# Graph network, one core: float32 rows turned whole, and no dense slot in the attention

## What is computed

```python
m = MLP(concat(x[dst], x[src] - x[dst]))          # 64 -> 64 -> 128 -> 64 -> 32, relu
x = layernorm(x + segment_mean(m, dst))
x = layernorm(x + segment_sum(x[src] * norm[src] * norm[dst], dst))      # no weights
x = layernorm(x + relu(norm_dst * segment_sum((x * norm_src)[src], dst) @ W + b))
for 3 layers:                                     # attention, 8 heads of 32
    e = leaky_relu((x @ Wl)[src] + (x @ Wr)[dst], 0.2)
    p = segment_softmax(sum(e * att), dst)        # per head
    x = batchnorm(mean_heads(segment_sum(p * (x @ Wl)[src], dst)) + bias (+ act) + x)
x = layernorm(x + ...)
```

## Time and profile before

| | us |
|---|---|
| median of 3 timed runs (5984.18 to 5997.32) | 5986.88 |
| span of the recorded execution | 7770.9 |
| PE busy (matmuls), share of the span | 5760.6 (74%) |
| POOL busy, share | 4059.1 (52%) |
| DVE busy, share | 3565.2 (46%) |
| ACT busy, share | 1748.7 (23%) |
| idle of POOL before attention gathers (2340) | 2221.5 |

### The profile page before, as it was taken

The page is one execution under the profiler, slowest core; times in us unless marked ns, Lnnn a source line. Parts: engine busy times, 40 slices in busy tenths (PEclk is TensorE's granted clock), DMA queues, the critical chain, the costliest instruction groups (busy, mean ns, idle before and its releaser), DMA issues.

```text
span 7770.9 us, 130521 instructions
## 1 busy us (share of the span) xinstructions
PE 5760.6 (74%) x43965; PEld 3691.2 (48%) x43965; DVE 3565.2 (46%) x6811; ACT 1748.7 (23%) x3748; POOL 4059.1 (52%) x4236
## 2 busy tenths in 40 slices
PE   5888886566646666578887876877787758788777
PEld 4666665455545454334444443444444424444444
DVE  5444444455544444444444444444444534444446
ACT  2222222344420000022222221222222122222221
POOL 4555554666646566455555533555555245555551
PEclk8888887777767776688888897888888878888988
DMA  4444443222212222233333332333333223333332
GB/s 103 129 129 129 128 128 98 51 56 56 56 47 56 55 56 55 49 82 93 88 91 88 89 85 56 90 90 89 92 89 89 80 58 92 89 89 93 91 88 65
DMA packets 688913, 648.23 MB, mean 83 GB/s; under 512 B 401396, under 2 KB 483771, under 8 KB 688251
## 3 DMA queue, kind: packets, MB, share of 16 engines
q1 hardware_dynamic: 548266, 463.96, 20.0%
q0 software_dynamic: 135616, 175.22, 11.8%
q10 hardware_dynamic: 4368, 0.70, 0.1%
HBM read 550.21 MB, written 89.17 MB: 82 GB/s over the span
## 4 chain that ended last, share of the span: by engine, by line
PE 43%; issue 22%; another core or an unknown queue 21%; DVE 9%; ACT 3%; DVEq 2%; DMA 0%; POOL 0%; ACTq 0%; POOLq 0%
PE ps L1055 14%; PE ps L900 7%; PE ps L994 5%; PE ps L1005 2%; PE ps L1015 2%; PE ps L855 2%; PE ps L915 1%; PE ps L980 1%; DVE region L1778 1%; DVE acc L1803 1%; PE ps L974 1%; PE ps L864 1%; ACT region L662 1%; PE ps L811 1%
## 5 line engine op out<-in xcount | busy, mean ns | idle before, releaser
L381 POOL DMA_INDIRECT rows<-table,idx x2340 | 2258.3, 965 | 2221.5 <-ACT region L651 1042.6
L1055 PE MATMUL ps<-region,hot 128*128 128x272 f32 x4992 | 1528.3, 457 | 295.8 <-DVE region L1756 159.4
L1055 PEld LDWEIGHTS ps<-region,hot 128*128 128x128 f32 x4992 | 1040.8, 219 | 690.9 <-issue 461.8
L1803 DVE TENSOR_TENSOR acc<-acc,ps 128x272 f32 x1248 | 544.5, 436 | 1685.6 <-remote 808.6
L662 ACT ACTIVATE region<-ps 128x512 f32<-128x512 f32 x1248 | 677.3, 595 | 2691.7 <-remote 1438.8
L900 PE MATMUL ps<-hot,region 128*128 128x192 bf16 (+1 forms) x6144 | 896.1, 309 | 444.2 <-issue 429.0
L900 PEld LDWEIGHTS ps<-hot,region 128*128 128x128 bf16 x6144 | 703.4, 123 | 590.9 <-issue 529.9
L368 POOL DMA_INDIRECT rows<-table,idx x728 | 696.6, 957 | 534.2 <-PE ps L835 320.4
L994 PE MATMUL ps<-xT,wcat 64*128 64x512 f32 x2496 | 771.8, 696 | 170.4 <-issue 92.1
L1778 DVE TENSOR_TENSOR region<-ps,region 128x1056 f32<-128x1056 f32 x582 | 724.7, 1251 | 44.0 <-issue 40.4
L398 POOL DMA_INDIRECT rows<-table,idx x576 | 546.6, 949 | 378.5 <-issue 157.3
(11 more groups left out here) (304 smaller groups left out, 6646.9 us busy)
## 6 DMA issues: line engine op xcount, KB each, us to landing
hot<-hot_dram SPq DMA_DIRECT2D x624, 256.0 KB
turned<-turned_dram SPq DMA_DIRECT2D x624, 128.0 KB
rows<-table,idx POOLq DMA_INDIRECT x3644
hot_dram<-hot SPq DMA_DIRECT2D x104, 512.0 KB
xwin<-table SPq DMA_DIRECT2D x1664, 24.0 KB
region<-hot_dram SPq DMA_DIRECT2D x64, 512.0 KB
region<-d_dram SPq DMA_DIRECT2D x104, 256.0 KB
turned_dram<-turned SPq DMA_DIRECT2D x104, 256.0 KB
```

The costliest lines, as they stand in the source:

```text
L381: pool.indirect_dma_start(rows[:, n % 2, j, :], None, table, bass.IndirectOffsetOnAxis(ap=idx[:, s:s + 1], axis=0)).then_inc(rows_in3[n % ...
L1055: mm = pe.matmul(ps[:, sum_bank(k, side, i), 0:PC + H], hot[:, b, 4 * side + 2 * i + j, :], px[b][:, 4 * side + 2 * i + j, :], start=(j == ...
L1803: v.tensor_tensor(at, at, ps[:, sum_bank(k, side, i), 0:PC + H], ALU.add).then_inc(att_added, 1)
```

## The change

- The rows that are gathered are plain float32: 32 channels, 128 B. In the edge network they come from the input `x`, in layer l of the attention from a new array `feats[l]` that SP stores as soon as x is given. The table keeps the three bfloat16 parts alone (`TAB` 80 to 48 words), for the windows, the dense reads and the convolution; ACT's copy into it goes.
- `rows` becomes a ring of 4 buffers (RING) of 8 places of 64 words: 32 channels and 32 zeros, cleared once by DVE. A slot j stands at `place(j)`, so that slots j and j + 4 lie side by side. One float32 transpose of 128 x 128 turns both sides of one slot pair onto their partitions and zeros between; four turn a group (`turn_rows`). After them the 12 window matmuls (`turn_windows`) write the partitions between, sides alternating.
- The dense slot of the attention goes: no `read_one`, `stationary_one`, `pick_one`, `numbers_for` there; POOL gathers 8 slots in each group. That of the edge network stays; DVE puts it straight into `rows`.
- In the edge network the gathers of group g wait for the turning of g - 4. In the attention they wait for the copy (`xs_kept`) of group n - 4 and, as before, for the turning (`x_made`) of n - 2.
- `x_made` and `x0_made` count 3 for a group in place of 4.

```diff
-TAB = C + 3 * C // 2
+TAB = 3 * C // 2
+RING = 4
+TURN = 3
...
-TURNS = [x for i in range(2) for x in [("row", 2 * i, 0), ("window", i, 0), ("row", 2 * i, 1), ("row", 2 * i, 2), ("window", i, 1),
-                                       ("row", 2 * i + 1, 0), ("row", 2 * i + 1, 1), ("window", i, 2), ("row", 2 * i + 1, 2)]]
+WINDOWS = [(side, i, s) for i in range(2) for s in range(3) for side in range(2)]
...
-        rows = sb("rows", [P, 3, 8, TAB])
+        rows = sb("rows", [P, RING, 8, 2 * C])
...
+        def place(j):
+
+            return 2 * (j % 4) + j // 4
...
         def pool_edges(pool):
 
-            pool.wait_ge(table_stored, 16)
+            pool.wait_ge(rows_cleared, 1)
             for g in range(G):
-                if g >= 3:
-                    pool.wait_ge(x0_made, 4 * (g - 2))
+                if g >= RING:
+                    pool.wait_ge(x0_made, TURN * (g - RING + 1))
                 for j in range(7):
                     pool.indirect_dma_start(
-                        rows[:, g % 3, j, :], None, table,
-                        bass.IndirectOffsetOnAxis(ap=idx[:, 8 * g + j:8 * g + j + 1], axis=0)).then_inc(gathered[g % 3], 16)
+                        rows[:, g % RING, place(j), 0:C], None, x,
+                        bass.IndirectOffsetOnAxis(ap=idx[:, 8 * g + j:8 * g + j + 1], axis=0)).then_inc(rows_at[g % RING], 16)
 
         def pool_attention(pool, l):
 
-            pool.wait_ge(table_stored, 16 * (l + 4))
+            pool.wait_ge(feats_stored, 16 * (l + 1))
             for g in range(G):
                 n = l * G + g
+                if n >= RING:
+                    pool.wait_ge(xs_kept, n - RING + 1)
                 if n >= 2:
-                    pool.wait_ge(x_made, 4 * (n - 1))
-                    pool.wait_ge(xs_kept, n - 1)
-                for j, s in enumerate(piece_slots(g)[0:8 - g % 2]):
+                    pool.wait_ge(x_made, TURN * (n - 1))
+                for j, s in enumerate(piece_slots(g)):
                     pool.indirect_dma_start(
-                        rows[:, n % 2, j, :], None, table,
-                        bass.IndirectOffsetOnAxis(ap=idx[:, s:s + 1], axis=0)).then_inc(rows_in3[n % 2], 16)
+                        rows[:, n % RING, place(j), 0:C], None, feats[l],
+                        bass.IndirectOffsetOnAxis(ap=idx[:, s:s + 1], axis=0)).then_inc(rows_at[n % RING], 16)
...
             for l in range(LAYERS):
+                sp.wait_ge(x_given, 3 + l)
+                sp.dma_start(feats[l].rearrange("(w p) c -> p w c", p=P), X[:, :, :]).then_inc(feats_stored, 16)
                 store_table(sp, 3 + l)
...
+        def turn_rows(pe, bank, b, made):
+
+            for j in range(4):
+                mm = pe.transpose(ps[:, bank, j * P:(j + 1) * P], rows[:, b, 2 * j:2 * j + 2, :].rearrange("p a c -> p (a c)"),
+                                  ident[:, :])
+            mm.then_inc(made, 1)
+
+        def turn_windows(pe, bank, b, made):
+
+            for side, i, s in WINDOWS:
+                q = 64 * side
+                mm = pe.matmul(ps[q + C:q + 2 * C, bank, 2 * i * P:2 * (i + 1) * P], xwin[:, b, 2 * side + i, s * C:(s + 1) * C],
+                               turned[:, b, (4 * side + 2 * i) * P:(4 * side + 2 * i + 2) * P], start=(s == 0), stop=(s == 2))
+                if i == 1 and s == 2:
+                    mm.then_inc(made, 1)
...
+                turn_rows(pe, XT, g % RING, x_made)
+                turn_windows(pe, XT, b, x_made)
...
-                if u >= 8 and u % 2 == 0 and u + 3 < G:
-                    if k > 0:
-                        pe.wait_ge(att_added, 4 * (l * G + k) - 1)
-                    read_one(u + 3)
```

More of the change, by code:

```diff
@@ L85, in build @@
         table = nc.dram_tensor("table", [W * P, TAB], F32).ap()
+        feats = [nc.dram_tensor(f"feats{l}", [W * P, C], F32).ap() for l in range(LAYERS)]
         turned_dram = nc.dram_tensor("turned_dram", [G, P, 8 * P], BF16).ap()
@@ L221, in build @@
               for k in range(2)]
-        rows4 = [rows[:, 0, :, :], rows[:, 1, :, :]] + [o0[:, 5120 + 640 * k:5120 + 640 * (k + 1)].rearrange(
-            "p (j c) -> p j c", j=8) for k in range(2)]
+        rows4 = [o0[:, 5120 + 8 * TAB * k:5120 + 8 * TAB * (k + 1)].rearrange("p (j c) -> p j c", j=8) for k in range(4)]
         parts4 = [r.rearrange("p j c -> p (j c)").bitcast(BF16).rearrange("p (j c) -> p j c", j=8) for r in rows4]
@@ L282, in build @@
         idx_made = sem("idx_made")
[L283 to L285 removed]
+        rows_at = [sem(f"rows_at{b}") for b in range(RING)]
+        rows_cleared = sem("rows_cleared")
+        feats_stored, x0_in = sem("feats_stored"), sem("x0_in")
         hot_made = sem("hot_made")
@@ L1296, in give_table @@
             def give_table(of, first=False):
-                hi, mid, lo = (tabparts[:, :, (2 + k) * C:(3 + k) * C] for k in range(3))
-                if first:
-                    cp(tab[:, :, 0:C], of)
-                else:
+                hi, mid, lo = (tabparts[:, :, k * C:(k + 1) * C] for k in range(3))
+                if not first:
                     v.sem_inc(x_given, 1)
@@ L1319, in _ @@
             v.memset(X[:, W - 1, :], 0.0).then_inc(x_zeroed, 1)
+            v.memset(rows[:, :, :, :], 0.0).then_inc(rows_cleared, 1)
             v.memset(zeros[:, :], 0.0).then_inc(zeros_made, 1)
@@ L1863, in attention @@
                         link(v.tensor_tensor(at, at, fscale[:, :].unsqueeze(2).broadcast_to([P, H, HK]), ALU.mult))
-                    def pick():
-                        if u % 2 == 0 and u + 3 < G:
-                            pick_one(l, u + 3)
-                    if phase in (3, 4) and u // 8 + 1 < CHUNKS:
-                        for q in range(2):
-                            stationary_one(l, u // 8 + 1, 2 * (phase - 3) + q)
                     if phase == 0 and ends:
```

185 lines of the change are left out of this document (25 added, 160 removed).

## The result

The change is slower. Its median is 6056.12 us (6048.3 to 6057.35), against 5992.1 for the kernel before on the same chip: ratio 1.0108, 95% interval 1.0093 to 1.0122. The forecast was 6070.

A forecast was written before the change was run, and what follows sets the result against it. POOL's gather issue was taken as the bound: floor 5892 us, plus 195 for 156 gathers, -9 edges, -11 layer starts, is 6067; 3 of waits gives 6070. Forecast's own range 6020 to 6160; 8 in 10, 5750 to 6160.

The forecast's parts named there:

- POOL's added gathers, 9.37 to 9.99 per group: Attention: without the dense slot POOL issues 156 more gathers at 1.249 us, 195 us; narrower rows win nothing in issue.
- The wait for n - 2 costs nothing: Attention: POOL's kept wait for the turning of group n-2 costs nothing while POOL is the bound.
- Landing, "about a microsecond", with PE ten microseconds later: Attention: the last row lands about a microsecond after issue, PE takes it up ten microseconds later, so landing is no bound.
- Dense read, -0.60 and up to 0.51 for the pick: Attention, PE per group: dropping the dense read saves 0.60 us, and the wait for DVE's pick at most 0.51.
- Turning, +0.5 (to +1.3): PE per group: transposes and windows take 1.42 to 2.16 us against 0.90; +0.5 was taken.
- Edges -9: Edge network: a ring of 4 lets POOL be one group further when PE starts, -9 us at most.
- Layer starts, -3.6 each: Attention layer starts: POOL waits for plain features, not the table; gathers start 3.6 us earlier, three times, -11 us.
- The sum: Whole kernel, timed run: 5892 + 195 - 9 - 11 = 6067 us, plus 3 of waits, forecast 6070.
- In a timed run POOL is issuing nearly all the time that it may.: Kernel before: POOL's gathers 5276 us plus 616 around them make a floor of 5892, the median only 95 above.
- The first rival: Attention: PE still paces timed runs; at a gather cadence of 1.15 us the change is faster, 5780 us; 40%.
- So the recording's excess is on PE, where instructions are small and many.: Recording of before: its 1784 us excess is PE stalls; the change's recorded span should fall to about 7070 us.
- The clock falls (3%): Attention: PE's granted clock falls from 0.87 to 0.70, a PE group is about 11.6 us, kernel near 6560; 3%.

The follow-up runs named there:

- with six: Six attention gathers per group, the others left out with their data: in the change 5810.75 us (0.9705), in the kernel before, dense slot kept, 5923.65 us (0.9893).

## Why the prediction was right, and where it was not

The runs fit a small model of one attention group, with PE and POOL side by side (us). Of POOL it has the gathers at 1.249 each; the longer ones among them add about 0.12 to a group.

| | PE's own pace, steady part | POOL's gathers | group, steady part | group, whole layer | time |
|---|---|---|---|---|---|
| before | 9.81 (with six) | 7.5, 9.37 | 9.82 | 9.77 | 5987 |
| before without dense slot | 9.81 - 0.68 = 9.13 (worked out) | 8, 9.99 | 10.31 | 10.30 | 6141 |
| change with dense slot | 10.20 (POOL not relieved) | 7.5, 9.37 | 10.20 | 10.12 | 6059 |
| change | 9.52 (with six) | 8, 9.99 | 10.12 | 10.10 | 6056 |
| change with 7.5 gathers | 9.52 | 7.5, 9.37 | 9.54 | 9.51 | 5872 |

Each steady group is the higher of PE's pace and POOL's gathers with the longer ones; the version without a dense slot has its late gathers on top.

PE's pace is its work and its waits. In the window from 2700 to 3500 us, per group: work 9.2 and waits 0.6 before, and the same with six; work 9.2 and waits 0.3 in the change with six; work 9.8 and waits 0.45 in the change with its dense slot. So the work that the reads take away, the turning gives back, and PE's gain of 0.3 is in its waits, above all that for DVE's pick (0.32 before).

Point by point, by the prediction's own steps:

- **POOL's added gathers, 9.37 to 9.99 per group.** Right as a mechanism: gathers 1.249 apart whatever the row's width, and the group at 10.10. The 0.11 more are gathers that last 1.0 to 1.9 us in place of 0.94: 37 us in the three layers, which the sum did not have.
- **The wait for n - 2 costs nothing.** Right: 6054.59 without it.
- **Landing, "about a microsecond", with PE ten microseconds later.** The second half did not carry over. In the change PE waits for the rows at two groups of three, and starts the turning 1.4 us or more, 1.9 in the median, after the last gather's end. That costs nothing only because POOL paces.
- **Dense read, -0.60 and up to 0.51 for the pick.** Right in range: 0.68 together in the steady part, 0.57 of it PE's work.
- **Turning, +0.5 (to +1.3).** Right as work: from its start to the next instruction's start 0.78 us before (own length 0.85; 0.83 with a dense slot in it) and 1.32 now, +0.54. In the group it comes to 0.39, since PE's waits get shorter beside it. In the prediction's working, 2400 columns in 1.20 give 1.54 for 3072, and not 1.48; at two at a time that is 0.77. A whole turning in the change's timeline of PE, in its two parts:

```profile
2908.61 0.66 PE L772 MATMUL ps<-ident,rows 128*128 128x128 f32 x4
2909.19 0.83 PE L780 MATMUL ps<-turned,xwin 128*32 128x256 bf16 x12
```

  The first and the last line of one in the timeline of before, recorded again (24 row and 12 window matmuls in all):

```profile
2900.78 0.23 PE L980 MATMUL ps<-identb,rows 128*32 128x128 bf16 x2
...
2901.35 0.28 PE L980 MATMUL ps<-identb,rows 128*32 128x128 bf16 x4
```

  The Trainium skill's "TensorEngine Tiling (Array Packing)", Key Properties and Restrictions, was weighed against it: tiles work side by side, and column tiling excludes the float32 transpose. The trace agrees: 4 transposes and 12 windows in two blocks take 1.41, where 36 packed matmuls, of more columns, took 0.85.
- **Edges -9.** Right: 941.3 to 931.8. (Over all recordings but the disturbed one it is 939 to 943 in versions of the kernel before and 932 to 937 in those of the change.)
- **Layer starts, -3.6 each.** Undersized: -5.8, -10.4 and -8.4. Of the 24.6 in all, 17.3 come back with the wait for the table's store; the other 7 go with ACT's copy and the wider store, which were not tried apart.
- **The sum.** It came within 14 us of the median because errors in it offset each other, so that closeness is luck. What held is that the change's attention runs at the pace of eight gathers per group. It put 605 us around POOL's stream and 5471 into it (4380 x 1.249), less 9 for the edges and 3 more for waits. The change has 519.5 around it and 5534 in it. The stages' gaps, read from a disturbed recording, were 85 too long, and POOL's stream 63 too short: 56 us for long gathers in all stages, and one wait of 10 us in the edge network.
- **"In a timed run POOL is issuing nearly all the time that it may."** This is the step that failed for the kernel before. It took the 95 us above the floor for slack. PE paced the attention: 9.81 in the steady part with POOL relieved, where the prediction had 9.1 plus 0.1 to 0.3, and 51% of the chain. Its 9.1 of work was close (9.2); what it left out of PE's group are the 0.6 that PE waits, half of it for the pick, which it had priced only as a saving. The first rival had said that PE paces, and was right about the kernel before; but it needed a shorter cadence (1.15) for the change to win, and the cadence is 1.249 everywhere. PE did gain 0.3 per group, the rival's -0.6 being too large; POOL's 8 x 1.249 then stood above PE's old pace as well.
- **"So the recording's excess is on PE, where instructions are small and many."** This failed outright. The recorded span was to fall from 7770.9 to about 7070 for this cause; it was 6053.5, and that of before, taken again, 5979.8. The stalls on "issue" and the low clock were of that one recording.
- **The clock falls (3%).** It did not: 1.00 in the attention, with four transposes in every group.

So the change took 0.3 us per group off PE's pace, which ruled, and gave 0.62 to POOL, whose 9.37, or 9.5 with the longer gathers, lay 0.3 below it in the steady part. The bound changed hands and came out 0.33 higher. What the new turning, the ring, the narrow rows and the early start win together (85 us) is real, but stands against 154 us for the dense slot.

On that bound, the Trainium skill's "Perfetto Trace Analysis", What "DMA-bound" means, names the issuing engine's sequencer as one of the things that can bound a kernel, and says that large descriptors then matter. The trace agrees with the first part: DMA engines are busy 0.39 in the window above, and POOL issues without a pause. On the second: with the same number of rows per gather, the size of a row changed nothing, as rows of 128 B, 320 B and 4 KB all took 0.94 us of POOL. What helped in these runs was fewer gathers.

## What to carry to other kernels

When two engines are level, price an edit on both of them, and compare the higher of the two before with the higher after; a saving on the one that leads is worth at most the distance to the second. To find each engine's own pace, relieve the other (here, leave out two gathers per group) rather than subtract idle time, and read the steady part of a stage apart from its start. And where the recorded span is far from the timed runs, record again before building on its stalls: the chain of waits of a clean recording showed in one line which engine paced.

## What was not expected of the hardware

- One recorded execution was 30% longer than all timed runs, with PE's granted clock at 0.87 in the attention and stalls on "issue" ahead of its small matmuls, while POOL kept its 1.249 us. The second recording of the same kernel had neither. What disturbed the first one was not found.
- Some gathers (147 of 2496 in the change's attention) last 1.0 to 1.9 us in place of 0.94: 37 us in all in the change's attention, 50 in the version that gathers 320 B rows and 42 before. What delays them was not tried.
- In the two convolution passes the granted clock and PE's busy share rose together: 0.80 in the change (1100 to 1600 us and 2100 to 2400), 0.85 to 0.88 in the change with 39 dense groups in the same stretches, 0.93 and 0.96 in the kernel before with 45 (1100 to 1450 and 1700 to 2000), where PE was busy 0.63 to 0.66, 0.72 to 0.77, and 0.79 to 0.84 of the window.
